# Moving a quarter of a recurrence's steps from an attention loop into the experts' loop

## What is computed

```
xn = layernorm(x)
s  = recurrence_0(xn);  f = experts_0(xn)          # layer 0
x  = x + s * silu(f)
xn = layernorm(x)
s  = recurrence_1(xn);  f = attention_and_experts(xn)   # layer 1
x  = x + s * silu(f)

recurrence_1, for each of 16 heads of 16 channels:
  r, k, v, g = projections of shifted mixes of xn;  w = exp(-exp(...))
  state = init;  for each token t:
      y[t]  = r[t] . (state + u * k[t] v[t]^T)
      state = w[t] * state + k[t] v[t]^T
  out = (silu(g) * layernorm_per_head(y)) @ oW^T

attention_and_experts:
  x2 = xn + causal attention (16 heads, latent of 32, rotary part of 32) of rmsnorm(xn)
  out = x2 + sum over the best 2 of 8 experts, and one shared expert, of rmsnorm(x2)
```

## Time and profile before

| | |
|---|---|
| Median of 3 runs | 2814.43 us (2812.1 to 2822.92) |
| Profiled execution, its own time | 2821.07 us |
| Span of the profiled execution | 2818.8 us |
| Instructions in the span | 36206 |
| Mean granted clock of TensorE | 0.887 |
| PE, DVE, ACT, POOL busy | 83%, 63%, 33%, 37% |

### The profile page before, as it was taken

The page is one execution under the profiler, slowest core; times in us unless marked ns, Lnnn a source line. Parts: engine busy times, 40 slices in busy tenths (PEclk is TensorE's granted clock), DMA queues, the critical chain, the costliest instruction groups (busy, mean ns, idle before and its releaser), DMA issues.

```text
span 2818.8 us, 36206 instructions
## 1 busy us (share of the span) xinstructions
PE 2332.4 (83%) x9640; PEld 1276.8 (45%) x9641; DVE 1768.5 (63%) x2977; ACT 924.0 (33%) x2467; POOL 1029.7 (37%) x986
## 2 busy tenths in 40 slices
PE   7887599996877987798789778978888797789778
PEld 3443366664434533443454345434534443454345
DVE  5777344443278658666855785477748566855777
ACT  2333123321235224412532352234225413522352
POOL 2113200001166146506622661265155416622661
PEclk9998799998778997898789888979997898889799
DMA  4341401003043014202410440143024203401430
GB/s 138 112 143 63 152 26 30 28 28 98 4 55 62 23 24 72 57 9 33 77 34 9 50 70 23 21 57 67 9 29 76 47 9 41 78 24 19 55 71 16
DMA packets 100043, 143.57 MB, mean 51 GB/s; under 512 B 7953, under 2 KB 61841, under 8 KB 99857
## 3 DMA queue, kind: packets, MB, share of 16 engines
q1 hardware_dynamic: 92370, 128.18, 23.1%
q0 software_dynamic: 3264, 8.93, 1.1%
q10 hardware_dynamic: 4224, 4.19, 0.4%
HBM read 50.94 MB, written 23.24 MB: 26 GB/s over the span
## 4 chain that ended last, share of the span: by engine, by line
issue 29%; PE 16%; DMA 11%; DVE 9%; POOL 8%; ACT 2%; DVEq 0%; POOLq 0%; ACTq 0%
DMA arena<-arena 11%; PE bank L1249 8%; DVE arena L1565 3%; POOL arena L1742 3%; POOL arena L1747 2%; DVE arena L1545 2%; PE bank L1139 2%; DVE arena L1558 2%; PE bank L1124 2%; PE bank L1165 2%; POOL arena L1749 1%; ACT arena L1372 1%; PE bank L1156 1%; ACT arena L1381 1%; PE bank L1147 1%
## 5 line engine op out<-in xcount | busy, mean ns | idle before, releaser
L1249 PE MATMUL bank<-arena 128*128 128x256 f32 (+2 forms) x1728 | 531.8, 468 | 6.4 <-DVE arena L1574 6.2
L1758 POOL TENSOR_TENSOR arena<-arena 128x512 f32<-128x512 f32 x256 | 370.1, 1446 | 291.7 <-issue 151.8
L1080 PE MATMUL bank<-arena 128*128 128x512 f32 (+2 forms) x896 | 423.9, 619 | 46.1 <-issue 18.6
L1372 ACT ACTIVATE arena<-bank,arena 128x128 f32<-128x128 f32 (+3 forms) x512 | 267.0, 526 | 545.5 <-DVE arena L1545 488.7
L1139 PE MATMUL bank<-arena 128*128 128x128 f32 x1280 | 257.4, 340 | 208.9 <-ACT arena L1381 207.5
L1249 PEld LDWEIGHTS bank<-arena 128*128 128x128 f32 x1728 | 331.8, 201 | 196.9 <-issue 153.3
L1565 DVE TENSOR_TENSOR_SCAN arena<-arena 128x512 f32<-128x512 f32 x256 | 375.8, 1468 | 0.0
L1139 PEld LDWEIGHTS bank<-arena 128*128 128x128 f32 x1280 | 186.2, 175 | 249.0 <-ACT arena L1372 213.5
L1080 PEld LDWEIGHTS bank<-arena 128*128 128x128 f32 (+2 forms) x896 | 159.7, 189 | 296.3 <-issue 255.4
L1124 PE MATMUL bank<-arena 64*128 64x128 f32 (+3 forms) x1024 | 257.3, 586 | 43.9 <-DVE arena L1524 26.9
L1558 DVE TENSOR_TENSOR arena<-arena 128x512 f32<-128x512 f32 x256 | 209.1, 817 | 77.0 <-DMA arena<-arena 76.7
(11 more groups left out here) (189 smaller groups left out, 2887.4 us busy)
## 6 DMA issues: line engine op xcount, KB each, us to landing
arena<-arena SPq DMA_DIRECT2D x256, 256.0 KB
arena<-in_L_attn_h SPq DMA_DIRECT2D x17, 512.0 KB, 3.6
arena<-in_W1T SPq DMA_DIRECT2D x8, 1024.0 KB, 5.8
arena<-in_W2T SPq DMA_DIRECT2D x8, 1024.0 KB, 8.8
sorted_rows<-arena SPq DMA_DIRECT2D x42, 128.5 KB, 9.0
arena<-sorted_rows SPq DMA_DIRECT2D x40, 128.5 KB, 2.1
gate_rows<-arena SPq DMA_DIRECT2D x39, 128.0 KB, 1.7
arena<-s_rows SPq DMA_DIRECT2D x9, 512.0 KB, 4.6
```

The source lines that it names most:

```text
L1080: last = nc.tensor.matmul(dst[0:rows, 0:width], w, x, start=(n == 0), stop=(n == len(pairs) - 1))
L1249: last = nc.tensor.matmul(dst[o], w, x, start=first, stop=last_one)
L1372: nc.scalar.activation(probs[s % PROBS][:, 0:n], bank[2 * (i % LAG) + half][:, 0:n], ACT.Exp, bias=neg_max[:, s:s + 1], accum_out=row_sum[ ...
L1758: nc.gpsimd.tensor_tensor(prods[n % PRODS], state[n % 2][:, 0:T], proj["r"][:, m, :], ALU.mult).then_inc(prod_done, 1)
```

## The change

1. **Units of the recurrence.** `UNIT_STEP` lists the steps with i % 4 != 3, 24 of the 32. Units 0 to 23 run in these; unit 0 and the outer product of unit 1 already run between the rotations q5 and q6. Units 24 and 25 run at the end of the attention loop, 26 after the `wo` reads, 27 before the read of `xc0`, and 28 to 31 in `between(0)` to `between(3)`. PE sums units 24 to 27 at expert 2 and 28 to 31 at expert 6. There are four state buffers in place of two.
2. **First column.** SP writes it with a DMA of 128 x 1 from the constant vectors (`first_column`) behind the copies on the same queue; POOL no longer does.
3. **Eviction.** `keep(i)` evicts the transposed blocks of both heads of a step with one activation, from banks 5 and 6 together; PE's transposes of the next step wait for it.
4. **Order to the gate.** `mean0` and six of the sixteen `wo` products stand before the last `weigh_values`. Mean and variance of group 1 go to bank 4, at expert 8 and after the last down product.
5. **End of a sequence.** The layer norm of group 1, the oW products (`gates`), the multiplication and the addition run inside the next sequence's projections, between their matmuls and mixes. The loop is cut anew: projections of sequence 0, then seven times attention and next projections, then the last attention and the rest. PE's projections wait for the lerp and, after the first product, for the last accumulation.
6. **Transfers.** The next sequence's loads stand between copies 28 and 29 on SP, behind a wait for the last value product; the gather stands behind product 26 on POOL. The last sequence no longer loads and prepares a ninth.
7. Buffers that shared memory (`xb`, `xbT`, `acc`, `y`, one of `hid`) have their own.

```diff
+STATES = 4
+UNIT_STEP = [i for i in range(PSTEPS) if i % NT != NT - 1]
+EARLY = len(UNIT_STEP)
...
+PRE_BANKS = [3, 5, 6, 7, 0, 1, 2]
+POST_BANKS = [2, 0, 1, 3, 5, 6, 7]
+LAST_BANK = 4
...
+            def first_column(b, n):
+                if n >= STATES:
+                    sp.wait_ge(prod_done, UNITS * b + n - STATES + 1)
+                sp.dma_start(state[n % STATES][:, 0:1], VEC["init"][:, n:n + 1]).then_inc(init_in[n % STATES], 16)
+
+            def sequence(b, last):
                 sp.wait_ge(a_read, pre.read(b, "pr_v1"))
+                for n in range(STATES):
+                    first_column(b, n)
                 for n in range(UNITS):
...
+                    copy_value(b, n)
+                    if n > STATES:
+                        first_column(b, n - 1)
+                    if n == EARLY + COPIES and not last:
+                        sp.wait_ge(pv_mm, GROUPS * b + 2 * GROUPS)
+                        load_sequence(b + 1)
+                first_column(b, UNITS - 1)
+                store_sequence(b)
...
-                    if s >= 2:
-                        pe.wait_ge(s_keep, STEPS * b + (s - 1))
+                    if i and half == 0:
+                        pe.wait_ge(s_keep, PSTEPS * b + i)
...
+            def gates(b, half):
+                pe.wait_ge(o_done, 2 * b + 2)
+                pe.wait_ge(last_read, 4 * b + 1 + 2 + half)
...
+            def before_attention(b, ended):
+
                 pe.wait_ge(lerp_done, b + 1)
...
+                    pe.wait_ge(v_read2, len(post.order["v"]) * b + 1)
...
                 lora_b(b, "v", "v", th[1])
+                if ended is not None:
+                    gates(ended, 0)
                 project(b, "k")
                 lora_b(b, "g", "g", th[1])
+                if ended is not None:
+                    gates(ended, 1)
...
+                    if i == PSTEPS + LAG:
+                        pe.wait_ge(y_read, 2 * b + 1)
+                        pe.wait_ge(s_exp, STEPS * b + STEPS)
+                        result("mean0", [(full, mean_m, y[:, 0, :], True, True)], bank[post.bank("mean0")])
+                        pe.wait_ge(y_out, GROUPS * b + GROUPS - 1)
+                        wo(0, 0, range(GROUPS - 1))
+                        wo(1, 0, range(GROUPS - 1))
...
-                    nc.scalar.activation(turned[h % HGROUP][:, 0:qt + 1, qt * P:(qt + 1) * P],
-                                         bank[5 + half][:, 0:(qt + 1) * P].rearrange("p (k c) -> p k c", c=P),
+                    nc.scalar.activation(turned_all[:, h % HGROUP:h % HGROUP + 2, 0:qt + 1, qt * P:(qt + 1) * P],
+                                         psum[:, 5 * T:7 * T].rearrange("p (h k c) -> p h k c", h=2, c=P)[:, :, 0:qt + 1, :],
                                          ACT.Copy).then_inc(s_keep, 1)
...
+                    if i in UNIT_STEP and i > 0:
+                        unit(b, UNIT_STEP.index(i))
...
+                    if i == PSTEPS:
+                        unit(b, EARLY)
+                    if i == PSTEPS + 2:
+                        unit(b, EARLY + 1)
+                        center()
...
+                    if e < 4:
+                        unit(b, EARLY + 4 + e)
+                    elif e == 4:
+                        ln_inv(b, 0)
+                    elif e == 5:
+                        read_out(b, 1)
+                        ln_scale(b, 0)
...
+                    if ended is not None:
+                        if x == "d":
+                            ln_inv(ended, 1)
+                        elif x == "r":
+                            ln_scale(ended, 1)
+                            ln_affine(ended, 1)
+                            ln_gate(ended, 1)
```

506 lines of the change are left out of this document (291 added, 215 removed).

## The result

The changed kernel takes 2941.45 us (median of 4 runs, 2930.26 to 2946.99), the kernel before 2813.26 us in the same comparison: a ratio of 1.0453, 95% interval 1.04 to 1.0506. It is slower by 128 us; the forecast was 2712 us. The profiled execution of the changed kernel has a span of 2945.2 us.

A forecast was written before the change was run, and what follows sets the result against it. No engine was always busy: DVE set the attention, PE the experts and projections. Per sequence -14.0 + 0 - 3.0 + 3.8 = -13.2 us, eight times, +4 us at the ends: 2719 us, taken as 2712 us; range 2640 to 2790.

The forecast's parts named there:

- the term that was put at nothing: Attention: the 32 one-column copies become transfers on the copies' queue, under 0.1 us each, counted as no cost.
- The slower rival: Small transfers keep copies slow: 5.9 us per copy and column, deciding from 5.3 us on; 2912 us, chance 0.07.
- Attention: Attention stretch per sequence: fewer scan pairs -17.2, moved first work -1.6, score waits +8, copy waits -3.2; together -14.0 us.
- score waits: Attention: DVE's waits for score matmuls rise to 14 us from 6.1, +8 us per sequence, bounds 0 and +16.
- the half clock: Attention rival with PE at half clock: the score chain costs +16 rather than +8; 2776 us, chance 0.13.
- Up to the gate: After the attention: PE work moved ahead or to the end saves 4.3 us, offset by +2.7, +0.4 and +1.2; sum 0.
- Experts: Experts' stretch: four pairs and three reads added to DVE, some work given away; DVE ends 3.8 us later per sequence.
- The rival of the locked port: Experts: five POOL products hold DVE up for their whole 1.44 us, +4 us per sequence; 2744 us, chance 0.17.
- From there to the next maximum: Sequence end and next projections: PE's dense products start earlier, lower-clock time partly regained, then projections +3.8 us for moved work.
- the first pair: Before the last two rotations: first scan and two outer products, 3.2 us, moved there, half hidden in DVE's idle time: -1.6 us.
- I take half of it back: End of a sequence: 3 us lost to PE's lower clock after the gap; half regained, -1.5 us.
- 11.5: Attention: groups of four steps were to take near 11.5 us, against 12.2 us read before the change.

The follow-up runs named there:

- e1: The changed kernel with the first column of each scan written by POOL again, as before: 2866.44 us, ratio to the kernel before 1.0204.
- f1: The kernel before with the values laid out so that a copy's 8 source rows lie 4 partitions apart: 2752.84 us, ratio 0.9791.
- f2: The changed kernel, column transfers included, with a copy's 8 source rows 4 partitions apart: 2851.84 us, ratio to the kernel before 1.0146.
- e16: e1 with an unused transfer of one 4-byte packet behind each copy on the same queue: 2872.94 us, ratio to the kernel before 1.0208.
- e21: e1 with an unused transfer of 16 packets of 4 bytes behind each copy: 2928.84 us, ratio to the kernel before 1.042.
- e5: e1 with the transposed probabilities of the two heads evicted apart again: 2836.67 us, ratio to the kernel before 1.0079.
- e17: The kernel before with only the single eviction of transposed probabilities per head pair: 2825.28 us, ratio 1.0048.
- e7: e1 with the first scan and first two outer products back behind the last rotation and first maximum: 2842.52 us, ratio to the kernel before 1.01.
- e12: e1 with two evictions, the first scan behind the rotations and DVE's loop closed behind the experts: 2821.4 us, ratio to the kernel before 1.0039.
- e18: e1 with 32 unused transfers of 128 x 4 bytes per sequence issued from ACT's queue: 3020.16 us, ratio to the kernel before 1.0747.

## Why the prediction failed

The measured time is 229 us over the forecast. 75 of them come from the term that was put at nothing, the column transfers; 154 come from terms of the sum that were sized wrong, since e1, without the columns, still takes 2866 us.

**The term at nothing.** "0.01 us each, so under 0.1 us for a transfer spread over 16 engines" priced the column by its own packets. That price holds: in the packet records 4 bytes take 9 ns. What the row of the window 306.4 to 307.6 could not show is what such a transfer does to its neighbours in the queue.

When the copies read 8 neighbouring partitions, a packet of 2048 bytes takes 312 ns in the median: 8 of them in 312 ns are 52.5 GB/s, the 51 to 53 of the windows. The Trainium skill, SBUF — State Buffer, section Door 1, puts such partitions on two ports of 27.2 GB/s, an estimate of 54 by that page; the trace agrees. In the kernel before the packets get shorter as the attention goes on: in sequence 2 the median is 312 ns in the first 10 us from the issue of the fifth copy on, and 164 to 191 ns in each 10 us from the 30th on. In the changed kernel it stays at 311 or 312. f1 and f2 show that what the copies read is the cause of the slow packets: with the rows 4 apart, they are short from the first on, with column transfers (109 ns in the mean) and without (107). That the engines drift into different copies, which read elsewhere, and that a transfer over all sixteen brings them back into step, fits e16, e21 and these two, but no record names a packet's engine: the drift itself is argued, not shown.

**Which way it went.** The slower rival had the right sign: copies kept at 5 us and more, "a product on POOL that waits for DMA". Its price was not the right one. It gave each column its 0.9 us of issue on top of a slow copy, 5.9 us in all, and 2912 us, with a chance of 0.07; measured are 5.2 us and 2941 us, and e16, where such an issue costs nothing, shows that the 0.9 us was not it. By its own threshold of 5.3 us the measured pace would about have decided nothing. It decided because the rest of the change had no gain to set against it, as e1 shows.

**The rest, term by term**, e1 against before per sequence, from the table:

- *Attention*: forecast -14.0 (-15.6 if the work moved ahead of the first maximum is counted out in full), measured -9.2. The pairs left as computed. The score waits were sized too small: 25 us a sequence (200 us in all) where I put 14, and 6.6 before; that is +18.4 for +8, beyond my bound of +16. A part of this was covered by luck: copy waits are gone in e1 (-9.6 where I put -3.2). The reason that I gave for the upper bound, the half clock, did not come: the granted clock of this stretch is 0.86 in e1 and 0.80 before. The single eviction is part of it: "ACT is busy for 58.7 of 114.6 us, so I count it at nothing" looked at ACT's time, but PE also waits until both banks are read; e5 gives 30 us back, of which its trace has about half here (2.1 of 4.9 us a sequence). In the kernel before it costs little or nothing (e17).
- *Up to the gate*: 0, measured +2.3; no run says where it comes from.
- *Experts*: DVE 3.8 us later, measured +4.3. Right, also that DVE then sets this stage. The rival of the locked port had 7.8 and is refuted.
- *From there to the next maximum*: -1.4 (-5.3 and -1.5 at the end, +3.8 for the projections, +1.6 for the first pair), measured +8.6. This is the largest miss. PE's dense products do start as early as forecast (5.2 us earlier against the accumulation's end; at 1276.13 in the changed kernel, before that end at 1277.5). But PE's last projection ends 64.4 us behind the accumulation in e1, 60.5 before, and the first maximum follows 9.2 us later, 4.5 before. For the first: the term "I take half of it back", of a stretch at the lower clock, had the wrong sign. That stretch grew from 3.4 to 12 us, an estimate of +4.3 us for an engine that is busy in it, where I put -1.5; at the same clock (6.8 us of it) the whole stretch is 4.9 us longer in place of 8.6. For the second: the first pair, "I take half as hidden: -1.6 us", costs 24 us in all by e7, since two rotations, POOL's part of them and the first maximum queue behind it. And I never priced the place of the branch: the earlier trace rows show an idle issue of 2.33 us on PE at it, on DVE it now lies where nothing covers it, 17.4 us of idle time in all.

The four differences are 6.4, 2.3, 0.5 and 10.0 us, eight times 19.2 is 154 us, which is e1 against the forecast (2866 and 2712); the columns add 75. The fit is closer than the numbers deserve, as the profiled execution of the kernel before is 8 us over its median. The groups of four steps take 12.4 us in e1 and 14.1 before, means over the seven intervals between 256-wide maxima; my single 12.2 of the earlier trace rows was the shortest of the seven, and so 11.5 was too low as well. Even in e12, with the first pair, the eviction and the branch put back, the stretch to the next maximum is 3.4 us longer than before and the experts 4.3, so that of the attention's 10.4 us little is left; which part of the moved tail costs these 3.4 us stays open.

## What to carry over

A small transfer must be priced by what it does to the transfers around it in the queue, too: look at whether the large transfers' packets are at their slow or their fast duration, and why. Before moving work off an engine to relieve copies, look at which partitions the copies read; here 8 source rows spaced 4 partitions apart were worth 2.1%. And when work or a loop's end is moved ahead of the first step of a chain, everything that the chain waits for behind it on that engine is moved too. Last, a stretch of one sequence is a sample: one group of four steps was the shortest of seven, and one and the same stage took 71.7 or 76.7 us with the clock.

## What was not expected of the hardware

- 256 unused transfers of 16 packets of 4 bytes cost 62 us in all, 256 of one packet 6 us, within the noise (e21 and e16 against e1).
- A packet of a copy takes half the time (107 for 221 ns in the mean) when the 8 source rows lie 4 partitions apart.
- At the end of a loop whose body takes some 260 us, the next instruction of DVE's program comes 2.7 to 3.1 us behind the branch in the kernel before, in e12 and in f2, and 5.6 us in e1 and the changed kernel, where slow copies run beside it. PE's branch has a record of 3.3 to 6.7 us in e1 (0.08 us the last time, when it is not taken), while products queued ahead of it still run. The Trainium skill, Advanced Engine Details and Errata, Control Flow Timing, gives a compare-and-branch 0.1 us. DVE's own branch record is 0.06 us, so the page is not against it; the time here lies behind the branch. For PE's record the measured one decides.
- A DMA issued from ACT costs ACT 990 ns in the median while the DMA engines are busy with the copies (e18).
